# Turning the second norm's tiles on VectorE and by copies inside SBUF instead of on TensorE

## The reference

```
x = x + _layernorm(_L0_attn_ref(_layernorm(x, axis=-1), ...), axis=-1)
x = x + _layernorm(_L0_ffn_ref(_layernorm(x, axis=-1), ...), axis=-1)

# _L0_attn_ref
s = jax.nn.sigmoid(jax.nn.silu(jnp.einsum('btd,hd->bth', x, s_w1) + s_b1) @ s_w2.T + s_b2)
u = (jnp.einsum('btd,sd->bts', x, B_w) + B_b) * s
def step(h, u_t):
    h = h @ A.T + u_t
    return (h, h)
y = jnp.einsum('bts,ds->btd', hs, C_w) + C_b + jnp.einsum('btd,ed->bte', x, D_w) + D_b
gate = jax.nn.sigmoid(jnp.einsum('btd,ed->bte', x, g_w) + g_b)
return y * gate

# _L0_ffn_ref
out_shared = _sq_relu(xf @ Ws1) @ Ws2
```

## Time and profile before

| | before |
|---|---|
| median of 3 runs | 839.78 us (839.55 to 840.52) |
| the profiled execution | 840.52 us, of which span 838.7 us |
| granted TensorE clock | 0.997 |
| TensorE busy | 810.8 us, 97% of the span |
| VectorE busy | 618.9 us, 74% |
| GpSimd busy | 399.8 us, 48% |
| ScalarE busy | 344.8 us, 41% |
| DMA engines, mean over 16 | 31% |

### The profile page before, as it was taken

One profiled execution on the slowest core, in us unless ns is written; L12 is line 12 of the kernel. 1 busy time (PEld: TensorE's weight loads), 2 busy tenths in 40 slices (PEclk: granted clock), 3 DMA queues, 4 the chain that ended last, 5 costly groups with the idle time before them and its releaser, 6 DMA issues. The chain is left out here.

```text
span 838.7 us, 11049 instructions
## 1 busy us (share of the span) xinstructions
PE 810.8 (97%) x3842; PEld 669.6 (80%) x3842; DVE 618.9 (74%) x1390; ACT 344.8 (41%) x555; POOL 399.8 (48%) x503
## 2 busy tenths in 40 slices
PE   5899999999999999999999999999999999999995
PEld 4778888888788878888788888888888887888873
DVE  5867885688867887687866888568886788744674
ACT  3533444353443444344443444434444344432343
POOL 1153546346445455354562554644644545625455
PEclk9999999999999999999999999999999999999998
DMA  8425203342234322262034420334223421122112
GB/s 289 163 60 193 100 17 144 143 151 101 79 123 147 112 94 101 101 240 99 13 126 144 184 100 30 145 128 151 101 95 107 155 96 51 51 101 101 51 51 101
DMA packets 23486, 95.18 MB, mean 113 GB/s; under 512 B 5123, under 2 KB 7555, under 8 KB 15622
## 3 DMA queue, kind: packets, MB, share of 16 engines
q1 hardware_dynamic: 22998, 94.27, 31.3%
q10 hardware_dynamic: 432, 0.20, 0.1%
HBM read 60.84 MB, written 33.61 MB: 113 GB/s over the span
## 5 line engine op out<-in xcount | busy, mean ns | idle before, releaser
L1870 POOL TENSOR_TENSOR xres<-work,xres 128x512 f32<-128x512 f32 x64 | 89.2, 1394 | 89.6 <-DVE work L1272 89.6
L470 PE MATMUL TM<-gw_hi,xT_hi 128*128 128x512 f32 x256 | 106.6, 416 | 0.0
L470 PE MATMUL TM<-dw_hi,xT_hi 128*128 128x512 f32 x256 | 100.7, 393 | 0.0
L472 PE MATMUL TM<-gw_hi,xT_lo 128*128 128x512 f32 x256 | 100.6, 393 | 0.0
L472 PE MATMUL TM<-dw_hi,xT_lo 128*128 128x512 f32 x256 | 100.2, 391 | 0.0
L471 PE MATMUL TM<-gw_lo,xT_hi 128*128 128x512 f32 x256 | 100.0, 391 | 0.0
L471 PE MATMUL TM<-dw_lo,xT_hi 128*128 128x512 f32 x256 | 99.6, 389 | 0.0
L1834 POOL TENSOR_TENSOR rsv<-rsv,negh 128x1 f32<-128x1 f32 x64 | 58.6, 915 | 65.5 <-DVE rsv L1268 65.1
L1874 POOL TENSOR_TENSOR work<-work,xres 128x512 f32<-128x512 f32 x62 | 79.1, 1291 | 10.5 <-ACT work L946 10.5
L946 ACT ACTIVATE work<-TM,nmz,rsz 128x512 f32<-128x512 f32 x62 | 48.3, 779 | 83.8 <-POOL nmz L1844 83.8
L1194 DVE TENSOR_TENSOR xin<-xin,norm_row 128x1024 f32<-128x1024 f32 x56 | 66.6, 1220 | 15.2 <-ACT norm_row L891 15.2
(11 more groups left out here) (171 smaller groups left out, 2109.4 us busy)
## 6 DMA issues: line engine op xcount, KB each, us to landing
xres<-in_x SPq DMA_DIRECT2D x16, 1024.0 KB, 5.9
x_scratch<-xres SPq DMA_DIRECT2D x16, 1024.0 KB, 3.9
xin<-in_x SPq DMA_DIRECT2D x15, 1024.0 KB, 5.2
out<-work SPq DMA_DIRECT2D x30, 512.0 KB, 3.4
xin<-in_x_t SPq DMA_DIRECT2D x14, 1024.0 KB, 6.1
rows_in<-ln_scratch SPq DMA_DIRECT2D x14, 512.0 KB, 5.3
xin<-in_x SPq DMA_DIRECT2D x2, 512.0 KB, 5.3
xres<-in_g_w_t SPq DMA_DIRECT2D x1, 1024.0 KB, 6.2
```

The source lines that it names most:

```text
L470: eng.matmul(ps, lhs[0], rhs[0], start=first, stop=False)
L472: return eng.matmul(ps, lhs[1], rhs[0], start=False, stop=last)
L1870: eng.tensor_tensor(xres[:, j, :], work[:, j, :], xres[:, j, :], ALU.add).then_inc(S["x1_ok"], 1)
```

## The change

For batches 0 to 6 the call `T` is gone from TensorE's lists. `x1_norm` writes the normed tile to `work` as before. Then `turn` on VectorE turns each of the tile's 64 blocks of 32x32 in one instruction and writes them to a new buffer `x2q` (two tiles, used in turn). `move` on ScalarE's queue issues four transfers inside SBUF for a tile (64 KB each), each of which takes 32 partitions of `x2q` to one quarter of the columns of `work`, spread over all 128 partitions. `t_hi` waits for the four landings and copies `work` to `x2T_hi` (instead of the PSUM bank), and `t_low` is now on GpSimd and subtracts in SBUF. Features come to lie on partitions in another order than before, so `W1f` gets its weights from a copy of `Ws1` whose rows are in that order, which is an additional input. The last batch keeps `T` and VectorE's `t_low`; there `x1_norm` writes its columns in the new order of features. All of `tail` and `body` is written in a new order, on all four compute engines.

```
-                T(*a, 0)
-                T(*a, 1)
...
+            def move(b, rep, j):
+
+                eng.wait_ge(S["turned"], body_at("turned", b, j))
+                for a in range(4):
+                    eng.dma_start(work[:, j, a * P:(a + 1) * P],
+                                  x2q[32 * a:32 * a + 32, j % 2, :].rearrange("r (q f) -> r q f", q=4))                       .then_inc(moved[j % 2], 16)
+
             def t_hi(b, rep, j):
-                eng.wait_ge(S["t_done"], body_at("t_done", b, j))
+                if rep == NB - 1:
+                    eng.wait_ge(S["t_done"], j + 1)
+                else:
+                    wait_moved(eng, b, j)
...
+                    eng.activation(by_blocks(x2T_hi[:, j % MS, :, :]), moved_tile(j), ACT.Copy).then_inc(S["t_hi"], 1)
...
+            def turn(b, rep, j):
+
+                eng.wait_ge(S["xn2_ok"], body_at("xn2_ok", b, j))
+                if b or j >= 2:
+                    wait_moved(eng, *divmod(b * L + j - 2, L))
+                eng.transpose(out=x2q[:, j % 2, :].rearrange("p (q k i) -> p q k i", q=4, k=KD),
+                              in_=work[:, j, :].rearrange("p (k q r) -> p q k r", q=4, k=KD)).then_inc(S["turned"], 1)
...
+            def t_low(b, j):
+                eng.wait_ge(S["t_hi"], body_at("t_hi", b, j))
+                eng.tensor_tensor(by_blocks(x2T_lo[:, j % MS, :, :]), moved_tile(j),
+                                  by_blocks(x2T_hi[:, j % MS, :, :]).bitcast(F32), ALU.subtract).then_inc(S["t_lo"], 1)
...
-                G(*a, 0, {2: 0})
-                scan_step(*a, 1)
-                W1f(*a, 1, 0, {2: 2})
...
+                G(*a, 0, {1: 0, 2: 1})
+                scan_step(*a, 2)
+                W1f(*a, 1, 0, {1: 3, 2: 4})
```

More of the change, by code:

```diff
@@ L16, with build @@
 ROUTE_GAP = 16.5
[L19 removed]
+def build(nc, x, xt, A, AT, BwT, Bb, CwT, Cb, DwT, Db, s1T, s1b, s2T, s2b, gwT, gb, Ws1p, Ws1, Ws2, W1, W2, Wr, eye, out):
     NB, T, D = x.shape
@@ L131, in build @@
         x_first = sem("x_first")
+        moved = [sem(f"moved{i}") for i in range(2)]
         chain = sem("dve_chain")
@@ L235, in build @@
         FM_RING = (2, ["w10", "w11", "h00", "h01", "b0", "s0", "w00", "w01", "h10", "h11", "b1", "s1"])
-        TR_RING = (2, ["t0", "t1", "t2", "t3", "t4", "t5", "t6", "t7"])
         HF_RING = (2, ["w10", "w11", "h00", "h01", "w00", "w01", "h10", "h11"])
-        for size, order in (TM_RING, FM_RING, TR_RING, HF_RING):
+        for size, order in (TM_RING, FM_RING, HF_RING):
             assert len(order) % size == 0
@@ L300, in build, with moved_tile, by_blocks @@
         q_wr = xres[:, 0, 0:KD * NE].rearrange("p (k n) -> p k n", n=NE)
+        def moved_tile(j):
+            return work[:, j, :].rearrange("p (a k i) -> p a k i", a=4, k=KD)
+        def by_blocks(xT):
+            return xT.rearrange("p k (a i) -> p a k i", a=4)
         def rows(t, i):
@@ L373, in _ @@
             load("c", CwT, D)
-            load("f1", tiles(Ws1), FH)
+            load("f1", tiles(Ws1p), FH)
             load("f2", tiles(Ws2), D)
@@ L1005, in body @@
                 ft_hi(*a, 5)
-                x1_norm(*a, 4)
+                move(*a, 4)
                 hidden(*a, 0, 0)
+                x1_norm(*a, 5)
+                ft_hi(*a, 6)
                 hidden(*a, 0, 1)
-                ft_hi(*a, 6)
-                x1_norm(*a, 5)
+                move(*a, 5)
+                t_hi(*a, 4)
                 ft_hi(*a, 7)
@@ L1013, in body @@
                 sig(*a, 1, 0)
-                t_hi(*a, 4)
+                t_hi(*a, 5)
                 zn(*a, 0)
-                t_hi(*a, 5)
                 sig(*a, 1, 1)
+                x1_norm(*a, 7)
                 zn(*a, 1)
-                x1_norm(*a, 7)
+                move(*a, 6)
+                move(*a, 7)
+                s_gate(*a, 1)
                 t_hi(*a, 6)
                 t_hi(*a, 7)
-                s_gate(*a, 1)
                 zn(*a, 2)
@@ L1473, in body @@
                 less_mean(*a, 0)
+                hs_low(*a, 2)
                 less_mean(*a, 1)
+                attn_norm(*a, 0)
                 scaled(*a, 0)
-                scaled(*a, 1)
-                attn_norm(*a, 0)
-                hs_low(*a, 2)
                 attn(*a, 1)
@@ L1515, in body @@
                 v_ag(*a, 4)
+                hs_low(*a, 5)
                 v_ep(*a, 4)
+                x1_ep(*a, 2)
                 less_mean(*a, 3)
-                hs_low(*a, 5)
+                x1_bn(*a, 3)
+                h1(*a, 0, 0)
                 attn_norm(*a, 4)
-                h1(*a, 0, 0)
-                x1_bn(*a, 3)
                 x1_ag(*a, 3)
+                turn(*a, 2)
                 x1_ep(*a, 3)
+                h1(*a, 0, 1)
+                hs_low(*a, 6)
+                x1_bn(*a, 4)
                 attn(*a, 5)
+                turn(*a, 3)
                 v_bn(*a, 5)
@@ L1581, in body @@
                 z_ep(*a, 3)
-                t_low(*a, 7)
             def last_tail(b, rep):
@@ L2031 @@
             give("in_x_t", a["x"].reshape(-1, P, 8, 4, P).transpose(0, 4, 2, 3, 1))
+        elif n == "Ws1_p":
+            w = a["Ws1"]
+            give("in_Ws1_p", w.reshape(-1, 4, 32, w.shape[1]).transpose(0, 2, 1, 3).reshape(w.shape))
         elif isinstance(n, tuple):
```

239 lines of the change are left out of this document (125 added, 114 removed).

## The result

The change made the kernel slower by 0.7%: 845.7 us (median; 840.7 to 849.2) against 840.0 for the kernel before, measured side by side; the ratio is 1.0067, 95% interval 1.0056 to 1.0077. I had predicted 820.1 and a range of 814 to 834. One of the 20 executions of the kernel before took 913.0 us and the other 19 took 839.3 to 840.7; why that one did, nothing here shows. The profiled execution's span is 844.9 us, 6.2 more than the span of before, 838.7.

A forecast was written before the change was run, and what follows sets the result against it. The prediction took TensorE's own work, plus 0.46 us of waiting a batch, to bound the kernel: 840.52 - 24.9 (transposes) + 5.2 (waits) = 820.8 us profiled, 820.1 median, range 814 to 834.

The forecast's parts named there:

- What is removed: TensorE's `T` transposes in seven batches: 28 pairs at 0.89 us, 24.9 us saved.
- What is added: Per batch, eight `turn` on VectorE, eight `t_low` on GpSimd (10.4 us), 32 DMA issues on ScalarE (14 us), plus landings.
- rival 1: `turn` on VectorE costs 1.22 us, adding 12 us of waits: 832 us; chance 0.08.
- rivals 2 and 3: Copies' landings of 3 to 4.1 us: 824 to 838, chance 0.15; of 5.6 us: 858.6, chance 0.08.
- four take 1.8 us: ScalarE's four DMA issues for one tile, from trace rows of 0.40 and 0.45 us each.
- (a): Start of `W1f` 0 0, needing `t_low` 3: no wait, room 0.3 us by count; 0.2 us taken.
- (b): Scan step 0 and `W1f` 1 0: scan wait 0 to 0.6 us, 0.3 taken; `W1f` 1 0 has room 0.8.
- (c): `H` 1 0, needing VectorE's `ft_low` 7: room 0.25 us, which one collision uses up; 0.3 us of wait taken.
- (d): Smaller places (`hs_low` 4 for `Y` 4, `h2` 1 1 for `W2` 4, scan steps 12 and 13): 0.4 us in all.
- The sum: TensorE's waits of 1.2 us less the existing 0.46, 0.74 a batch, seven times: 5.2 us added.
- waits twice as large, 828.5: Upper bound given for the time, with TensorE's predicted waits doubled: 828.5 us.
- Rival 3: Path through the copies becomes the bound; at landings of 5.6 us, 43.7 us more waits, 858.6 us; chance 0.08.

The follow-up runs named there:

- the first experiment: The changed kernel with all of `move`'s DMA issues on SyncE's queue instead of ScalarE's: 828.05 us, ratio 0.985 to the kernel before.

## Why the prediction was wrong

**What is removed** was right: 224 instructions are gone from TensorE, the 24.9 us that I gave them close the account above, and it is TensorE that set the time before.

**What is added.** `turn` 0.69, measured 0.70; rival 1 (1.22) is out, and so is the estimate of 1.24 from the Trainium skill's page "VectorE: DVE Perf Modes", section "The three transpose paths". The measured price is near the 0.68 to 0.69 of the 128x512 instructions from which I took it. `t_low` 1.30, measured 1.30. Landing 2.1, median 2.1 and at most 3.5: rivals 2 and 3 as they were worded, with landings of 3 and more, are out. The step that failed is **ScalarE's issues**. The term "four take 1.8 us" came from rows of loads at the kernel's start, 0.40 and 0.45; measured is 0.625, so 2.5 us a tile and 20 us a batch where I had 14. And at place (a) the term stood once where two tiles' issues are in one row.

The Trainium skill's page "DMA: Bandwidth & Descriptors", section "Issuing engines are not separate DMA queues", weighs the sequencer's time against the transfer's: "usually small". The trace speaks against it here: one issue is 0.625 us against a landing of 2.1, four are 2.5, and the 17.7 us of the first experiment are the cost of that time in the wrong stream.

**The places.** (a) `W1f` 0 0: predicted 0.2 us, measured 1.96 in most batches. Counted from `B` 0, which began at 400.1 (the wanted start of `W1f` 0 0, 407.6, less the 7.5 of the prediction), I had tile 3's issues end at 3.3; they ended at 5.9. I had counted four issues behind `turn` 3, as if `move` 2 had been over by then. In the code both stand behind `x1_norm` 3, and the profile shows all eight in one row from 400.84: at 0.45 each they would have ended at 4.3, 1.0 too late by the count, and the price adds the other 1.6. (`turn` 3 ended at 2.3 and not at 1.5, so 0.8 of the 1.0 would have been there with four issues too.) After that `t_hi` 3 ended at 8.6 (I had 5.9) and `t_low` 3 at 9.9 (7.2). In this batch the last landing took 2.7 us, in the other six at most 2.3; that is why its wait is 2.45 and not 1.96. (b) Scan step 0: I took 0.3 out of 0 to 0.6, measured 0.75 to 0.9 in four batches, 1.5 and 2.1 in two others; the eight issues were in the count, at 0.45 each, and began along with `x1_norm` 7, earlier than I had them. 8 x 0.175 is 1.4 us more than the 0 to 0.6 that I had, and the long single issues make the 1.5 and the 2.1. `W1f` 1 0 had room, as said. (c) `H` 1 0: predicted 0.3, and there is no wait. (d) The smaller places: 0.4 in all, but `Y` 4 alone takes 0.85 and once 2.0; I had put `hs_low` 4 within 0.3 of its time. It isn't a matter of this step's place alone: in all six kernels that moved it, the other waits grew by as much or more.

**The sum** was 5.2 us of added waits; they are 25.8. Even with the issues off ScalarE it was too low: the waits of the SyncE version are 14.7 us, 11.5 more than before. Its 828.05 lies in the range of 814 to 834, but 8 us above the forecast, since (d) was too small and (a) isn't ScalarE's alone.

**What wasn't in the prediction at all** is the clock, 4.2 us: TensorE that waits can lose more than the wait. 1.2 of them, and 0.5 us of a longer wait of `T` for `x1_norm`, lie in the last batch, which I had called unchanged. And the bound "waits twice as large, 828.5" was a factor on a number, not a bound on its terms. With an issue of 0.625 in the counts as they stood, (a) becomes 0.4 and (b) 1.0 to 2.0, and the time 826 to 833, still in the range. With the issues at (a) ending at 5.9, (a) becomes 2.3, and the time 840 to 847. So it took the price and the count together. **Rival 3** named the right mechanism, that the path through the copies becomes the bound, but hung it on the landing alone; I gave it 0.08. It should have had a second form, by the length and the number of the issues.

## What to carry to other kernels

A DMA costs the engine that issues it time in its own stream, 0.6 us for the transfers inside SBUF here, and what counts is what stands behind it: price it from a steady-state row of the same kind, since rows of other transfers (0.34 to 0.45 here) can mislead, count every issue that stands in one row with it, and put it on a queue that computes nothing; that one move was worth 17.7 us here. Work taken from the bounding engine is a gain only as far as the others were early: a filler as large as the saving, put where the engine waits, tells in one run whether it was. Where a step moved forward carries the wait to the next consumer, as VectorE's low parts did in every kernel here that moved them, suspect the stretch as a whole, though the shares of the engines that compute beside TensorE are far from full.

## What the runs showed of the hardware

The issue of a 64 KB transfer inside SBUF took 0.625 us on ScalarE (median; 550 to 1987 ns) and 0.603 on SyncE (542 to 1941), with 128 pieces of 512 bytes. With 32 pieces of 2 KB it took 0.612 on ScalarE. ScalarE's loads at the start of the kernel before took 0.40 to 0.45, SyncE's stores of 512 KB in the changed kernel 0.337.

TensorE's clock went from 2.4 to 1.2 GHz (granted 0.58 over 4 us) directly behind single waits in the steady state, with matmuls 0.43 us apart for some 3 us. It did so after three of the changed kernel's waits, one of them in the last batch, and with `s_gate` 1 moved after twelve: five of the seven new ones, six of the seven ahead of `W1f` 0 0, and the one in the last batch. It never did where fillers took the waits' place. What tells the waits with a fall from those without, I can't say: by the view's lengths one of 2.64 us had none, one of 1.78 us had one, and the waits ahead of `W1f` 0 0 are of like length in both kernels, with two falls in one and six in the other.

Executions of the changed kernel spread over 1% (840.7 to 849.2), those of the kernel before over 0.2% but for one: here the kernel that waits in many places repeats less well than the one bound by one engine.
